# A cross product in two column tiles of TensorE, batch beside batch, with its last two chunks by column halves

## The reference

```python
def fake_quant(x, scale, zp):
    q = jnp.clip(jnp.round(x / s + z), 0.0, 255.0)
    return (q - z) * s
...
x = x + jnp.matmul(fake_quant(_layernorm(x), s1, z1), fake_quant(ctx, s2, z2))
x = x + attention(_layernorm(x))     # qkv_w 1024 x 3072, out_w 1024 x 1024
x = x + ffn(_layernorm(x))
```

## Time and profile before

| | us |
|---|---|
| median of three runs | 621.76 |
| lowest and highest run | 621.49, 622.23 |
| span of the profiled execution | 620.4 |
| TensorE products busy | 601.3 (97%) |
| VectorE busy | 472.8 (76%) |
| ScalarE busy | 292.3 (47%) |
| the cross product's last step of the first pair on TensorE ends, about | 30 |
| first dense product | 39.54 |

### The profile page before, as it was taken

One profiled execution on the slowest core, in us unless ns is written; L12 is line 12 of the kernel. 1 busy time (PEld: TensorE's weight loads), 2 busy tenths in 40 slices (PEclk: granted clock), 3 DMA queues, 4 the chain that ended last, 5 costly groups with the idle time before them and its releaser, 6 DMA issues.

```text
span 620.4 us, 12885 instructions
## 1 busy us (share of the span) xinstructions
PE 601.3 (97%) x4937; PEld 310.6 (50%) x4937; DVE 472.8 (76%) x938; ACT 292.3 (47%) x366; POOL 11.5 (2%) x17
## 2 busy tenths in 40 slices
PE   3898999999999999999999999999999999999998
PEld 1463454455455545554555455545545554454455
DVE  6899998788659965987596769659964789867661
ACT  5887695865464546534644554464431243110010
POOL 3000010000000000000000000000000000000000
PEclk9999999999999999999999999999999999999999
DMA  8999995861464175226712671464241042232311
GB/s 319 387 386 361 388 365 205 277 208 69 165 220 161 69 254 193 95 81 258 266 71 97 207 237 68 161 217 130 102 136 35 1 172 102 85 119 85 114 55 53
DMA packets 38912, 108.14 MB, mean 174 GB/s; under 512 B 3802, under 2 KB 4186, under 8 KB 38880
## 3 DMA queue, kind: packets, MB, share of 16 engines
q1 hardware_dynamic: 37744, 104.35, 47.5%
q0 software_dynamic: 992, 3.18, 1.5%
q10 hardware_dynamic: 144, 0.18, 0.2%
HBM read 99.30 MB, written 8.39 MB: 174 GB/s over the span
## 4 chain that ended last, share of the span: by engine, by line
PE 84%; DVE 5%; SPq 4%; DMA 4%; ACT 1%; issue 1%; ACTq 0%; DVEq 0%
PE dense L1259 16%; PE dense L1261 16%; PE dense L1260 16%; PE cross L1308 7%; PE turn L1250 6%; PE dense L1426 4%; PE dense L1427 4%; PE dense L1428 4%; DVE wq L860 4%; PE score L1387 2%; SPq L600 2%; DMA wq<-in_qkv_w 2%; PE score L1413 2%; DMA raw<-in_ctx 2%; PE dense L1442 1%; PE cross L1473 1%
## 5 line engine op out<-in xcount | busy, mean ns | idle before, releaser
L1259 PE MATMUL dense<-wq,xn_h 128*128 128x512 f16 x400 | 151.9, 380 | 0.0
L1260 PE MATMUL dense<-wq,xn_h 128*128 128x512 f16 x400 | 151.6, 379 | 0.0
L1261 PE MATMUL dense<-wq,xn_l 128*128 128x512 f16 x400 | 151.6, 379 | 0.0
L351 ACT ACTIVATE code<-raw,cst,qc 128x1024 uint8<-128x1024 f32 x72 | 87.7, 1235 | 6.7 <-DMA raw<-in_ctx 6.5
L1308 PE MATMUL cross<-code,q1t 128*128 128x512 f16 x256 | 73.4, 387 | 3.0 <-DVE xa L867 1.4
L1261 PEld LDWEIGHTS dense<-wq,xn_l 128*128 128x128 f16 x400 | 39.1, 98 | 47.2
L1259 PEld LDWEIGHTS dense<-wq,xn_h 128*128 128x128 f16 x400 | 39.1, 98 | 41.5 <-issue 1.6
L1260 PEld LDWEIGHTS dense<-wq,xn_h 128*128 128x128 f16 x400 | 39.2, 98 | 38.2
L351 ACT ACTIVATE code<-lnt,cst,qc 128x1024 uint8<-128x1024 f32 x32 | 39.6, 1239 | 28.4 <-DMA lnt<-in_ctx 25.4
L906 DVE SCALAR_TENSOR_TENSOR at<-cst,score 128x512 f32<-128x512 f16 x24 | 16.4, 683 | 37.4 <-PE score L1387 37.2
L1426 PE MATMUL dense<-wo,rope 128*128 128x512 f16 x112 | 42.5, 379 | 0.0
(11 more groups left out here) (204 smaller groups left out, 992.6 us busy)
## 6 DMA issues: line engine op xcount, KB each, us to landing
raw<-in_ctx SPq DMA_DIRECT2D x72, 512.0 KB, 4.5
lnt<-in_ctx SPq DMA_DIRECT2D x32, 512.0 KB, 4.2
wo<-in_ctx SPq DMA_DIRECT2D x16, 512.0 KB, 8.6
wo<-in_qkv_w SPq DMA_DIRECT2D x12, 512.0 KB, 11.7
wq<-in_qkv_w SPq DMA_DIRECT2D x8, 512.0 KB, 11.9
x_scratch<-xa SPq DMA_DIRECT2D x8, 512.0 KB, 3.0
wq<-x_scratch SPq DMA_DIRECT2D x8, 512.0 KB, 3.7
wq<-in_ctx SPq DMA_DIRECT2D x7, 512.0 KB, 11.7
```

The costliest lines, as they stand in the source:

```text
L351: act.activation(low_bytes, src, ACT.Identity, scale=qc[:, 1:2], bias=z2).then_inc(s_u8, 1)
L1259: pe.matmul(bank[:, :], a_h[:, k, :], w_hi, start=(k == 0 and not started), stop=False)
L1260: pe.matmul(bank[:, :], a_h[:, k, :], w_lo, start=False, stop=False)
L1261: ins = pe.matmul(bank[:, :], a_l[:, k, :], w_hi, start=False, stop=(k == KC - 1 and not last))
```

## The change

The first pair's chunks alternate between the two batches: chunk 2k is tile k of batch 0, chunk 2k + 1 tile k of batch 1. A step `first_cross(kc)` takes both. The stationary side has 64 columns, and the output goes to rows 0 to 63 of a bank for batch 0 and to rows 64 to 127 for batch 1, so that each product takes one of two column tiles of TensorE. In place of the column of ones there are two further products for each batch and bank, with the constant 128 - z1 (its float16 part and the rest) in all 64 columns. One evacuation of 128 rows for each column half is left, the first with its bn_stats ahead of the second. Chunks 14 and 15 both come in two column halves, in the order 14 left, 15 left, 14 right, 15 right; VectorE makes the codes of 14 right, ScalarE those of 15 right. The products of constants are 4 behind each of steps 4, 5 and 6; WARM stays. VectorE has three more small steps ahead of `s_qc`, on which ScalarE's first chunk waits.

```diff
+        shift = lw[:, 0, 0:1].bitcast(F16)
+        step = lw[:, 1, 1:2]
...
+            def last_codes():
+                c = CHUNKS - 1
+                act.wait_ge(s_clast[1], 16)
...
+                act.activation(low_bytes, chunk0_stage(c)[:, 1, :], ACT.Identity, scale=qc[:, 1:2], bias=z2).then_inc(s_u8last, 1)
...
             for c in range(4, CHUNKS):
                 quantise(0, c)
+            last_codes()
             for j in range(6):
                 weight_hi(j)
...
+                    sp.dma_start(chunk0_stage(c), ctx_v[0, c % 2, c // 2, :, :].rearrange("p (a n) -> p a n", a=2)).then_inc(s_ctx0[c], 16)
...
-            for c in range(4, CHUNKS):
+            for c in range(4, CHUNKS - 2):
                 load_chunk(0, c)
+            for n in range(2):
+                for c in range(CHUNKS - 2, CHUNKS):
+                    sp.dma_start(chunk0_stage(c)[:, n, :], ctx_v[0, c % 2, c // 2, :, n * NT:(n + 1) * NT]).then_inc(s_clast[c % 2] if n else s_ctx0[c], 16)
...
             def half_codes(c):
-                dve.wait_ge(s_clast if c == CHUNKS - 1 else s_ctx0[c], 16)
+                dve.wait_ge(s_clast[0], 16)
...
+            def first_cross_evac(n):
+
+                cols = slice(n * NT, (n + 1) * NT)
+                if n:
+                    dve.wait_ge(s_cmm, CHUNKS)
+                else:
+                    dve.wait_ge(s_cbank, 1)
+                return dve.scalar_tensor_tensor(xa[:, cols], X[n][:, :], step, xa[:, cols], ALU.mult, ALU.add)
+
+            def first_norm2():
+                link(first_cross_evac(0))
+                dve.bn_stats(st[:, 0, :], xa[:, 0:NT])
+                first_cross_evac(1).then_inc(s_ce, 2)
+                dve.wait_ge(s_ce, 2)
+                link(dve.bn_stats(st[:, 1, :], xa[:, NT:DM]))
+                rstd(XSC)
...
+            link(dve.tensor_copy(step, qc[:, 2:3]))
+            link(dve.tensor_copy(shift[:, 0:1], qc[:, 5:6]))
+            link(dve.tensor_tensor(shift[:, 1:2], qc[:, 5:6], shift[:, 0:1], ALU.subtract))
             dve.tensor_tensor(qc[SEQ:P, 2:3], qc[SEQ:P, 2:3], qc[SEQ:P, 5:6], ALU.mult).then_inc(s_qc, 1)
...
             bias_low()
-            cross_evac(0, 0)
             bias_rows_set()
             x_shift(1)
             half_codes(CHUNKS - 2)
-            half_codes(CHUNKS - 1)
-            cross_evac_last()
-            norm2(0)
+            first_norm2()
             weight_lo(0)
...
+            def first_cross(kc):
+
+                if kc == 0:
+                    pe.wait_ge(s_ah, 2)
+                pe.wait_ge(s_u8, 2 * kc + 2)
+                for n in range(2):
+                    if n and kc == KC - 1:
+                        pe.wait_ge(s_u8half, 1)
+                        pe.wait_ge(s_u8last, 1)
+                    for part in range(3):
+                        for b in range(2):
+                            lhs = q1t[:, kc, b, 0, :] if part == 0 else shift[:, part - 1:part].to_broadcast([P, SEQ])
+                            ins = pe.matmul(X[n][b * SEQ:(b + 1) * SEQ, :], lhs, code[:, (2 * kc + b) % RING, n * NT:(n + 1) * NT],
+                                            start=(kc == 0 and part == 0), stop=(kc == KC - 1 and part == 2))
+                            if n and part == 2:
+                                ins.then_inc(s_cmm, 1)
+                    if n == 0 and kc == KC - 1:
+                        ins.then_inc(s_cbank, 1)
...
-            pe.wait_ge(s_ones, 1)
-            for n in range(CHUNKS):
-                chunk(0, n)
-                if n < KC:
-                    constants(16 if n == KC - 1 else 3)
+            for kc in range(KC):
+                first_cross(kc)
+                if kc == 2:
+                    pe.wait_ge(s_ones, 1)
+                if 3 < kc < KC - 1:
+                    constants(4)
             next_codes(1)
```

More of the change, by code:

```diff
@@ L184, in build @@
         s_cmm = sem("s_cmm")
-        s_clast = sem("s_clast")
+        s_clast = [sem(f"s_clast{n}") for n in range(2)]
+        s_u8last = sem("s_u8last")
         s_cbank = sem("s_cbank")
@@ L351, in quantise @@
                 act.activation(low_bytes, src, ACT.Identity, scale=qc[:, 1:2], bias=z2).then_inc(s_u8, 1)
+            def last_codes():
+                c = CHUNKS - 1
+                act.wait_ge(s_clast[1], 16)
+                low_bytes = code[:, c % RING, :].bitcast(U8T).rearrange("p (a n b) -> p a n b", a=2, b=2)[:, 1, :, 0]
+                act.activation(low_bytes, chunk0_stage(c)[:, 1, :], ACT.Identity, scale=qc[:, 1:2], bias=z2).then_inc(s_u8last, 1)
             def x_high(i, e):
@@ L594, in load_chunk @@
             def load_chunk(i, c):
[L595 to L598, removed]
                 if isinstance(i, int) and i == 0:
-                    sp.dma_start(chunk0_stage(c), ctx_v[0, c // KC, c % KC, :, :].rearrange("p (a n) -> p a n", a=2)).then_inc(s_ctx0[c], 16)
+                    sp.dma_start(chunk0_stage(c), ctx_v[0, c % 2, c // 2, :, :].rearrange("p (a n) -> p a n", a=2)).then_inc(s_ctx0[c], 16)
                     return
@@ L845, in norm2 @@
                 mean_rstd(x_rows(i)[:, :], XSC)
[L846 to L850, removed]
+                dve.tensor_scalar(lnt[:, :], x_rows(i)[:, :], mv[:, 0:1], nw[:, 0:1], ALU.subtract, ALU.mult).then_inc(s_xn, 1)
             def x_low(i, e):
@@ L867, in cross_evac @@
                 dve.scalar_tensor_tensor(x_rows(i)[rows, :], XX[SEQ:P, :], qc[SEQ:P, 2:3], x_rows(i)[rows, :], ALU.mult, ALU.add).then_inc(s_ce, 1)
[L869 to L882, removed]
+            def first_cross_evac(n):
[12 more added lines that the diff above has]
+                rstd(XSC)
+                dve.tensor_scalar(lnt[:, 0:NT], xa[:, 0:NT], mv[:, 0:1], nw[:, 0:1], ALU.subtract, ALU.mult).then_inc(s_xnhalf, 1)
+                dve.tensor_scalar(lnt[:, NT:DM], xa[:, NT:DM], mv[:, 0:1], nw[:, 0:1], ALU.subtract, ALU.mult).then_inc(s_xn, 1)
             def rotate(i, j):
@@ L1303, in chunk @@
                 for n in range(2):
[L1304 to L1307, removed]
                     ins = pe.matmul(X[n][:, :], lhs, code[:, c % RING, n * NT:(n + 1) * NT],
```

## The result

The changed kernel takes 626.18 us (median of 6, 624.41 to 627.03) against 621.86; the ratio is 1.0064, with a 95% interval of 1.0053 to 1.0076. The forecast was 621.8 and no change. Its profiled span is 624.9 us against 620.4: 4.5 us more. One run of a later kernel was slow (785.07 us, granted clock 0.758) and counts in no comparison.

What follows compares the result with a forecast made beforehand. The bound was the chain through the sync queue and sixth weight to ScalarE's x_high. The norm's gain and the later products each counted 0, leaving span 620.4, plus 1.36 to the median: forecast 621.8, range 621.1 to 623.1.

Steps and rivals of the forecast that it cites:

- The chain and its slack: First 60 us: sixth weight's landing and rounding hold x_high; cross product and norm lie beside, about 1.06 us to spare.
- (a): Evacuation and norm behind the cross product: two 128-row evacuations at 0.74 us replace four, bn_stats at 0.66.
- (b): Opening on VectorE: three more small steps ahead of s_qc delay a_high and ScalarE's codes by 0.57 us.
- (d): What follows the cross product: aggregate at 33.4, x_turn(0) at 37.99, 0.3 us of slack left, span unchanged.
- (c): Cross products on TensorE: a pair of 64-column tiles overlaps and costs 0.216 us; the cross product ends 1.03 us later.
- the first two rivals: Cross product: a pair's tiles run one after the other (+8.4 us, chance 0.04), or their weight loads don't overlap (+6.7, 0.03).
- The rule of the Trainium skill: TensorE: a weight load overlaps running products only when the row groups differ; it would give 628.5 us.
- rows 9: Profile rows before the change: value products on four 32-column tiles, products and loads 10 ns apart, taken as showing overlap.
- The clock rival: Cross product: half-wide products do not raise TensorE's clock near 20 us; +9 us, 630.8, chance 0.04.
- The span stays 620.4: Whole kernel: norm gain and later products both count 0 on the path, so the profiled span does not change.
- The fourth: TensorE's tail around the cross product grows more than counted: up to 1.24 us, chance 0.15; beyond, some 623.4, 0.04.
- The 0.15 for slower: Whole kernel: total chance of a loss beyond 0.2% (1.24 us), summed from four slower cases of 0.04, 0.03, 0.04, 0.04.

Runs made afterwards that it cites:

- with the norm let through and shorter warming: Changed kernel with x_high(0, 0) and (0, 1) ahead of weight_hi(5) and warming products of 24x192 and 11x512 columns: 620.59 us, ratio 0.9979.
- the kernels with the shorter stop: The changed kernel (626.18 us), its repeat (625.55 us) and the kernel before with 113 warming products of 126 columns instead of 74 of 192 (624.50 us).

## Why the prediction was wrong

**The chain and its slack: right.** That the cross product, its evacuation and the norm were beside the chain, with about 1.06 us to spare, is borne out from both sides. The changed stage costs nothing once the program length is put back (ratio 1.0000), and with the norm let through and shorter warming the ratio is 0.9979. In the kernel before with 39 products more the constants landed later, `x_turn(0)` came at 37.98 instead of 37.25, and `x_high` still at 38.95.

**The parts (a) and (b): right.** The evacuation by L881 took 0.75 and 0.73, and the aggregate came at 33.36 when the constants landed early. The three small steps delayed the opening as counted: from the landing of the constants to the start of `a_high` it is 9.10 us in the changed kernel, 8.51 before. In the first profile of the changed kernel the constants landed 0.62 later than before, and `x_turn(0)` came 0.64 later than forecast: 38.63 against 37.99. I had no term for how far that landing scatters; it moved `x_high` by 0.36 us there. One slip in (d) changes nothing: T[1] is full at 39.1 by the working's own numbers (37.99 + 1.11) and not at 38.9; the slack of 0.3 us is the one to 39.1.

**The part (c): right.** Durations of the new products in the changed kernel (ns min/median/max, first and last start), and two groups of its timeline:

```profile
L1329 PEld LDWEIGHTS cross<-code,q1t x32: 106/110/177, 16.1 to 30.7; 128*64 128x64 f16 x32
```

```profile
20.05 0.38 PE L1329 MATMUL cross<-code,q1t 128*64 128x512 f16 x2
20.26 0.60 PE L1329 MATMUL cross<-code,lw 128*64 128x512 f16 x4
20.69 0.38 PE L1329 MATMUL cross<-code,q1t 128*64 128x512 f16 x2
```

Three pairs in 0.64 us are 0.213 for a pair, which I had at 0.216. Two tiles of 128x64 run side by side and their loads of 0.11 lie under products on the same rows, so the first two rivals are out. The rule of the Trainium skill that I weighed (TensorE: Matmul & The Clock Gate, Part 3) does not hold here, as rows 9 had suggested. The clock rival is out too: with nothing but the new pairs on TensorE the clock rose, at 18.8 us in this profile. Over the nine profiles with the changed cross product it rose at 18.1 to 20.9, over the three with the old one at 20.0 to 20.6, so that it came sooner in this one says nothing.

**The step that failed** is the one that closed part (d): "The span stays 620.4". It costed the 64 new products and the 25 products of constants that go by the time that they take on TensorE, and at the spot alone. It did not cost the 39 pairs of instructions (product and load) by which the rest of TensorE's program moves. None of the rivals was of that kind. The fourth, which let the end of the cross product slip, had the sign but not the cause: the cross product ended when it should. Where the prediction has no change of the span, the runs show a loss that goes with these 39 pairs alone: 4.3 us in the changed kernel (626.18 against 621.86), 2.8 in the kernel before with the same 39 added (624.50 against 621.73), none with the 39 taken out again (ratio 1.0000). The profile of before had a trace of it in the row of the instruction queue (21 packets, 0.34 MB), and the burst of small products at 83 us stood in rows 9, where I used it for another question. That the burst makes this place tender is likely, by the order of events, and was not tried.

**The chances.** The 0.15 for slower held no share for TensorE's program growing by 78 instructions ahead of a dense burst of them. Whether a given length meets a stop is partly luck: 39 and 49 products more did, 29 more and none did not. The time lies 3.1 us above the range.

## What to carry to other kernels

A change that adds or takes instructions moves every later instruction of that engine against the blocks in which they are fetched; a stop with no releaser but issue, far behind the edit and just behind a burst of small instructions, is the sign, and a run that changes only the number of filler products, with their columns kept, tells it from the change's own cost. Here ten filler products fewer took some 4 us off the changed kernel, and ten more added some 3. The mean granted clock of every run belongs beside such a profile: two executions of one program with the same stop can differ by the clock behind it. And a gain beside the chain stays unseen until what hides it moves: the changed kernel was faster than the kernel before only when ScalarE took the rows ahead of the last weights.

## What the runs showed of the hardware

- TensorE stopped for 2.15 to 3.75 us behind the 600th or 601st recorded product of its program, whatever the products ahead were, and went on at 89.0 to 89.4 us in all four profiles with a stop. Why the fetch is not made sooner (the DMA engines are full at 407 GB/s there) was not tried and stays open.
- In all four profiles the clock was at the 1.2 GHz level for 3.4 us, from 88.9, 89.8, 90.0 and 90.5 us on, while TensorE still stood or 0.6 to 1.2 us after it went on. In the changed kernel that made a stop of 2.3 us one of 4.1. In seven of fifteen runs of the kernels with the shorter stop the granted clock stayed at 1.000, and they took 624.00 to 625.03 us instead of 625.80 to 627.03.
- Pairs of 128x64 products on two column tiles ran 0.213 us apart with 512 columns at the high clock level, as full products do (0.21).
- The landing of the first small transfer (the constants) scatters between 4.95 and 5.87 us from run to run and shifts the opening with it.
